# Two transformer blocks on one core: who subtracts, who reads a head, and where block 1's first gelus stand

## The chip, the cores and the metric

The kernel runs on one core of one Trainium2 chip. The metric is the device time of one execution in microseconds. Three runs of the kernel before took 2537.11, 2530.70 and 2521.50 us, a median of 2530.7. The engines are named in the profile as PE (TensorE, with PEld for its weight loads), DVE (VectorE), ACT (ScalarE), POOL (GpSimd) and SP (SyncE, which issues transfers).

## The reference, cut to what matters

Eight sequences of 512 rows by 512 columns go through two blocks. Block 0 quantizes activations and weights; block 1 works on them in full precision.

```python
# block 0, 16 heads of 32 columns
xn = adaln(x, c, g1, w_ada1, b_ada1)
q, k, v = split_heads(bitlinear(xn, w_qkv, b_qkv))
attn = softmax(einsum('bhqd,bhkd->bhqk', q, k) * hd ** -0.5)
o = einsum('bhqk,bhkd->bhqd', attn, v)
x = x + bitlinear(o, w_proj, b_proj)      # bitlinear: act_quant(o) needs each row's absolute maximum
h = gelu(bitlinear(adaln(x, c, ...), w_fc1, b_fc1))
x = x + bitlinear(h, w_fc2, b_fc2)
# block 1, one head of 512 columns
h = film(rmsnorm(x), cond);  x = x + softmax(Q(h) K(h)^T / sqrt(512)) V(h) @ proj
h = film(rmsnorm(x), cond);  x = x + gelu(h @ mlp_w1 + b1) @ mlp_w2 + b2
```

## The kernel before, in words

Every engine has a program of its own, and semaphores tie them together. Each program calls `both(i, j)`: block 0 of sequence i and block 1 of sequence j = i - 1 side by side. It is called nine times: once with block 0 alone, seven times in full, and once with block 1 alone. Nothing is planned at run time: the order on every engine is written out by hand.

Block 0's attention is cut into 64 tiles, four chunks c of four heads, each head with four tiles of 128 keys by 512 queries. The order is a list of 88 slots (c, n): chunk 0 has 24 slots, in which only scores by query run (for the maxima), and chunks 1 to 4 have 16 slots each. In slot (c, n) of the latter, the scores by key of tile e = 16(c - 1) + n are made (`scores_by_key`, line 1035), ScalarE takes their exponential in fp32 (`exponential`, line 1042), and the upper halves of these fp32 words are used as the bf16 high part. The rest, exponential minus high part, is rounded to bf16 by `prob_low` (line 1046) on GpSimd or on VectorE, as the lists `LOW_POOL` and `LOW_DVE` say. Before, VectorE has one of four tiles in the first three chunks and three of four in the last, 24 in all; GpSimd has 40. Scores by query (line 991) and their maxima (`maxima`, VectorE, line 997) run 24 tiles ahead, up to slot (3, 7). Exponentials lie in a ring of eight tiles; every fourth of them waits until the product of the head that used these places is done.

When a head's four tiles are ready, TensorE multiplies them with the head's values (`weigh_values`, line 1061, 32 matmuls of 66 columns), at the slot that `VALUES_AT` gives: `VALUE_LAG` slots after the head's first tile. The two parts of the result and the sum of the exponentials lie in bank 4. VectorE reads them one slot later (`read_head`, lines 1069, 1076 and 1078): reciprocal of the sum, both parts times it, and one part plus the other into y. After the last head it takes absolute maxima of y (`amax0`, line 829) and their scales; ScalarE rounds (`round0`, line 847), VectorE subtracts the constant (line 855), TensorE transposes (line 863), ScalarE copies (line 869) and TensorE projects (`proj0`, line 1087). Then come the norm, whose gain operations are line 814 on VectorE, and block 0's dense layers.

Block 1 uses banks 6 and 7 alone, in turn. Pieces of it are placed between slots: its last scores and projections at chunk 0 and the start of chunk 1, its second norm (`SQUARE_AT`, `NORM_AT`), the turning of the normed rows (`TURN_AT`, lines 1262, 1281, 1291, 1287) and, by `M_AT`, the first six jobs of the list M. M is 16 products of its first dense layer ("fc1") and 16 of its second ("fc2"); each is 12 matmuls of 512 columns (lines 1213 to 1215). A first-layer product is followed by a gelu on ScalarE (line 1430), a bf16 copy on VectorE (line 1436) and its rest on GpSimd (line 1441). There are two buffers for gelus, and a gelu waits for the rest of the one before the last. Exponential and gelu need different tables in ScalarE, so a table load stands before each change. The jobs of M behind the first `M_IN` stand after the attention, mixed with block 0's work. GpSimd also adds block 1's second bias (line 1255) beside four of them.

Of the kernel before, what the change touches and what calls it, by code (L numbers as in the profile page):

```python
# [6 lines left out]
ALU = mybir.AluOpType  # L7
ACT = mybir.ActivationFunctionType
# [5 lines left out]
P = 128  # L14
# [13 lines left out]
MEMORY = 53120  # L28
# [45 lines left out]
LATE_HIGH = {(0, 5): ("q", 2), (0, 9): ("k", 2), (1, 4): ("q", 3), (1, 8): ("k", 3)}  # L74
LATE_LOW = {(0, 7): ("q", 2), (0, 11): ("k", 2), (1, 5): ("q", 3), (1, 9): ("k", 3)}

VALUE_LAG, READ_LAG = ((8, 6, 6, 7), 1)
# [29 lines left out]
LOW_DVE = [e for e in range(KC * HEADS) if (e % 4 == 3 if e < 3 * HEADS else e % 4 != 0)]  # L107
# [68 lines left out]
def two_blocks(nc, a, out):  # L176
# [6 lines left out]
    with ExitStack() as ctx:  # L183
# [73 lines left out]
        o_parts = qk_f[:, 0, 0:TT * 2 * HD].rearrange("p (t s d) -> p t s d", t=TT, s=2)  # L257
# [10 lines left out]
        sum_inv = fp32(2, TT)  # L268
# [56 lines left out]
        o_ok = signal("o_ok", H)  # L325
# [497 lines left out]
        def amax0(dve, i, c, tiles=range(TT)):  # L823
            for t in tiles:
                if c == 1:
                    dve.wait_ge(o_ok.sem, o_ok(i, H))
                else:
                    dve.wait_ge(y_full.sem, y_full(i, c // 2 * TT + t + 1))
# [236 lines left out]

        def read_head(dve, i, h):
            b = ready(dve, plan0, ("o", h), i)
            o = banks[:, b, 0:TT * 2 * LOW].rearrange("p (t s n) -> p t s n", t=TT, s=2)
            dve.reciprocal(sum_inv[:, h % 2], o[:, :, 0, HD]).then_inc(o_small.sem, 1)
            if h > 0:  # L1070
                dve.wait_ge(o_ok.sem, o_ok(i, h))
            else:
                dve.wait_ge(lo_ok.sem, lo_ok(i, 2 * KC - 1))
            dve.wait_ge(o_small.sem, o_small(i, h + 1))
            r = sum_inv[:, h % 2].unsqueeze(2).unsqueeze(3).to_broadcast([P, TT, 2, HD])
            dve.tensor_tensor(o_parts, o[:, :, :, 0:HD], r, ALU.mult).then_inc(free[b].sem, 1)
            done(dve, plan0, ("o", h), i)
# [987 lines left out]
```

## Time and profile before

| | |
|---|---|
| median of three runs | 2530.7 us |
| profiled execution | 2516.55 us |
| its span, first to last instruction | 2514.7 us |
| mean granted TensorE clock | 0.923 |
| PE busy | 2120.9 us, 84% |
| DVE busy | 1683.9 us, 67% |
| ACT busy | 1225.0 us, 49% |
| POOL busy | 768.5 us, 31% |

Busy time is a share of the whole span. The seven full passes of the loop are alike; one of them, whose first exponential starts at 1314.80 us and whose next pass starts its scores at 1563.9 us, is looked at closely below. A granted clock of 1.00 is TensorE's 2.4 GHz, 0.50 is 1.2 GHz, and a number between them is a mean over a stretch.

### The profile page before, as it was taken

To read this page: it belongs to the slowest core of one execution; us is meant where nothing else is said; L and a number is where in the kernel's file an instruction comes from. 1 tells how busy PE (TensorE), PEld (TensorE's weight loads), DVE (VectorE), ACT (ScalarE), POOL (GpSimd) and SP (SyncE) were. 2 spreads that over 40 slices of the span, in tenths; PEclk is the share of its full clock that TensorE was granted. 3 is DMA by queue.
4 is the path that set the end of the run, shared out by engine and by line. 5 is a ranking of instruction groups with operands and counts; after the bars stand their busy time and mean duration, and the time that the engine had idled before them with its cause. 6 is when DMAs were issued, how large, how long until landed. Compare 5 with 4: busy or idle time off the path is not lost.

```text
span 2514.7 us, 40181 instructions
## 1 busy us (share of the span) xinstructions
PE 2120.9 (84%) x13525; PEld 1069.9 (43%) x13525; DVE 1683.9 (67%) x2870; ACT 1225.0 (49%) x2032; POOL 768.5 (31%) x684
## 2 busy tenths in 40 slices
PE   4667688878997799779997899789988898789989
PEld 3424344444444444344444444344444344444434
DVE  4578645877578666877578756967587757866422
ACT  6535334474436554464446544564447444574330
POOL 0135101353125422353125412343136312452112
PEclk8777888989999899989999899989999899999989
DMA  7554111302230122202230213102231213101202
GB/s 276 192 181 164 59 51 34 94 18 76 78 113 22 52 75 96 83 18 76 85 105 22 76 51 121 58 29 82 85 97 31 71 60 124 34 35 51 101 23 95
DMA packets 85507, 200.82 MB, mean 80 GB/s; under 512 B 7604, under 2 KB 48856, under 8 KB 73120
## 3 DMA queue, kind: packets, MB, share of 16 engines
q1 hardware_dynamic: 77512, 174.91, 20.6%
q10 hardware_dynamic: 7776, 23.07, 2.6%
q8 instruction: 127, 2.08, 0.3%
q14 instruction: 92, 0.75, 0.1%
HBM read 161.97 MB, written 35.72 MB: 79 GB/s over the span
## 4 chain that ended last, share of the span: by engine, by line
PE 55%; DVE 17%; issue 13%; ACT 10%; POOL 2%; DMA 2%; ACTq 1%; DVEq 0%; SPq 0%; POOLq 0%
PE banks L1213 10%; PE banks L1214 10%; PE banks L1215 10%; PE banks L1170 5%; PE banks L1105 5%; DVE memory L997 4%; PE banks L1061 4%; DVE memory L1046 2%; ACT memory L1042 2%; DVE memory L814 2%; PE banks L991 2%; PE banks L900 1%; ACT L1042 1%; ACT memory L847 1%; PE banks L1035 1%
## 5 line engine op out<-in xcount | busy, mean ns | idle before, releaser
L1213 PE MATMUL banks<-memory 128*128 128x512 bf16 x1536 | 599.8, 390 | 46.9 <-DVE memory L1463 26.6
L1214 PE MATMUL banks<-memory 128*128 128x512 bf16 x1536 | 597.3, 389 | 0.0
L1215 PE MATMUL banks<-memory 128*128 128x512 bf16 x1536 | 595.3, 388 | 0.0
L1046 POOL TENSOR_TENSOR memory<-memory 128x512 bf16<-128x512 f32 x320 | 356.3, 1125 | 499.2 <-ACT memory L1042 497.4
L1042 ACT ACTIVATE memory<-banks 128x512 f32<-128x512 f32 x512 | 283.9, 597 | 216.7 <-PE banks L1035 179.8
L997 DVE TENSOR_REDUCE memory<-banks 128x1 f32<-128x512 f32 x512 | 330.2, 679 | 52.0 <-PE banks L991 51.0
L1441 POOL TENSOR_TENSOR memory<-memory 128x512 bf16<-128x512 f32 x128 | 163.2, 1275 | 512.5 <-DVE memory L1436 512.5
L991 PE MATMUL banks<-memory 96*128 96x512 bf16 x512 | 197.2, 415 | 103.8 <-DVE memory L997 94.4
L1213 PEld LDWEIGHTS banks<-memory 128*128 128x128 bf16 x1536 | 153.6, 100 | 242.0 <-DVE memory L1463 35.0
L1061 PE MATMUL banks<-memory 128*128 128x66 bf16 x4096 | 177.7, 209 | 76.6 <-DVE memory L1046 67.0
L1215 PEld LDWEIGHTS banks<-memory 128*128 128x128 bf16 x1536 | 153.6, 100 | 192.3 <-issue 19.2
L1035 PE MATMUL banks<-memory 98*128 98x512 bf16 x512 | 202.9, 425 | 30.3 <-ACT memory L1042 23.3
L1214 PEld LDWEIGHTS banks<-memory 128*128 128x128 bf16 x1536 | 153.7, 100 | 174.4 <-issue 16.0
L1061 PEld LDWEIGHTS banks<-memory 128*128 128x128 bf16 x4096 | 165.5, 108 | 120.5 <-issue 109.1
L1046 DVE TENSOR_TENSOR memory<-memory 128x512 bf16<-128x512 f32 x192 | 172.0, 916 | 18.9 <-ACT memory L1042 18.7
L1463 DVE TENSOR_TENSOR memory<-banks,memory 128x512 f32<-128x512 f32 x128 | 88.2, 689 | 141.6 <-PE banks L1215 140.7
L1436 DVE CAST memory<-memory 128x512 bf16<-128x512 f32 x128 | 73.0, 571 | 156.8 <-ACT memory L1430 155.4
L847 ACT ACTIVATE memory<-memory 128x512 f32<-128x512 f32 x96 | 61.3, 710 | 183.4 <-DVE memory L840 177.2
L1162 ACT ACTIVATE memory<-banks 128x512 bf16<-128x512 bf16 x128 | 69.4, 596 | 152.1 <-PE banks L1156 152.1
L1430 ACT ACTIVATE memory<-banks,memory 128x512 f32<-128x512 f32 x128 | 86.9, 684 | 113.2 <-PE banks L1215 112.7
L991 PEld LDWEIGHTS banks<-memory 96*128 96x128 bf16 x512 | 52.2, 102 | 192.1 <-DVE memory L997 152.4
L1170 PE MATMUL banks<-memory 128*128 128x512 fp8e4 x512 | 120.8, 391 | 9.1 <-ACT memory L1162 9.1
(169 smaller groups left out, 3115.9 us busy)
## 6 DMA issues: line engine op xcount, KB each, us to landing
memory<-weight_parts SPq DMA_DIRECT2D x80, 1024.0 KB, 4.9
memory<-head_parts SPq DMA_DIRECT2D x192, 128.0 KB, 2.7
head_parts<-memory SPq DMA_DIRECT2D x64, 256.0 KB, 2.2
weight_parts<-memory ACTq DMA_DIRECT2D x10, 1024.0 KB, 5.0
memory<-in_L_cond_w_fc SPq DMA_DIRECT2D x2, 4096.0 KB, 14.3
memory<-in_x SPq DMA_DIRECT2D x32, 256.0 KB, 3.2
memory<-ada_rows SPq DMA_DIRECT2D x16, 512.0 KB, 4.6
memory<-in_L_cond_mlp_w ACTq DMA_DIRECT2D x8, 1024.0 KB, 8.8
```

The lines of the kernel that those rows point to most:

```text
L991: pe.matmul(banks[:, b], q_stack[0:STACK, c % STACKS, j, t * P:(t + 1) * P], k_stack[0:STACK, c % STACKS, j], start=True, stop=True).then_ ...
L997: dve.tensor_reduce(neg_max[:, c % 2, t, j:j + 1], banks[:, b], AX.X, ALU.max, negate=True).then_inc(free[b].sem, 1)
L1035: pe.matmul(banks[:, b], k_stack[0:rows, c % STACKS, j, kt * P:(kt + 1) * P], q_stack[0:rows, c % STACKS, j], start=True, stop=True).then_ ...
L1042: act.activation(expo[:, e % RING], banks[:, b], ACT.Exp, scale=HEAD_SCALE).then_inc(free[b].sem, 1)
L1046: eng.tensor_tensor(prob_lo[:, e % RING], expo[:, e % RING], prob_hi[:, e % RING], ALU.subtract).then_inc(ok.sem, 1)
L1061: mm = pe.matmul(banks[:, b, at:at + VALUE], part[:, (h * TT + kt) % RING, t * P:(t + 1) * P], values[:, kt, h], start=(kt == 0 and part i ...
L1105: mm = pe.matmul(banks[:, b], xq[:, k, t * P:(t + 1) * P], w0_fc1[:, k, n * D:(n + 1) * D], start=(k == 0), stop=(k == KC - 1))
L1170: mm = pe.matmul(banks[:, b], hid_q[:, f], w0_fc2[:, f], start=(f == 0), stop=(f == FC - 1))
L1213: pe.matmul(bank, lh, rh, start=(k == 0), stop=False)
L1214: pe.matmul(bank, lh, rl, start=False, stop=False)
L1215: mm = pe.matmul(bank, ll, rh, start=False, stop=(k == KC - 1))
L1441: pool.tensor_tensor(hidden_half(g)[:, 1, m], wide[:, f % 2], hidden_half(g)[:, 0, m], ALU.subtract).then_inc(g1_lo.sem, 1)
```

## The change

The lists of rests become contiguous: GpSimd has tiles 0 to 40, VectorE tiles 41 to 63. When a head's product is done, ScalarE copies its high part into y (`copy_head`), one slot after the product; VectorE keeps the reciprocal of the sums in a column for each head and adds the low part out of the bank. After the last head four operations multiply y by the reciprocals of all heads (`divide0`), and the absolute maxima wait for each. Of block 1's list M, two products stand in the attention instead of six, at (4, 5) and (4, 11), and no gelu, bf16 copy or rest of them: these come after the attention on their engines. GpSimd's four additions of block 1's bias stand beside jobs 0 to 3 of M instead of jobs 6 to 9. Some places in the tables shift by one to three slots.

```diff
-LATE_HIGH = {(0, 5): ("q", 2), (0, 9): ("k", 2), (1, 4): ("q", 3), (1, 8): ("k", 3)}
-LATE_LOW = {(0, 7): ("q", 2), (0, 11): ("k", 2), (1, 5): ("q", 3), (1, 9): ("k", 3)}
-VALUE_LAG, READ_LAG = ((8, 6, 6, 7), 1)
+LATE_HIGH = {(0, 5): ('q', 2), (0, 9): ('k', 2), (1, 4): ('q', 3), (1, 9): ('k', 3)}
+LATE_LOW = {(0, 6): ('q', 2), (0, 12): ('k', 2), (1, 5): ('q', 3), (1, 9): ('k', 3)}
+VALUE_LAG, COPY_LAG, READ_LAG = ((6, 7, 7, 7), 1, 1)
+FIRST_DVE = 41
+COPY_AT = {later(at, COPY_LAG): h for at, h in VALUES_AT.items()}
-M_AT = ((3, 0), (3, 4), (3, 8), (3, 12), (4, 0), (4, 6))
+M_AT = ((4, 5), (4, 11))
-TURN_AT = ((2, 4), (2, 6), (2, 8), (2, 10))
+TURN_AT = ((2, 7), (2, 9), (2, 11), (2, 13))
-MAX_AT = {(0, 19): 0, **{(c, 10): c for c in range(1, KC)}}
-HIGH_AT = {(0, 17): 0, **{(c, 9): c for c in range(1, KC)}}
-LOW_AT = {(0, 17): 0, **{(c, 11): c for c in range(1, KC)}}
-LOW_DVE = [e for e in range(KC * HEADS) if (e % 4 == 3 if e < 3 * HEADS else e % 4 != 0)]
+MAX_AT = {(0, 19): 0, (1, 8): 1, (2, 10): 2, (3, 10): 3}
+HIGH_AT = {(0, 17): 0, (1, 9): 1, (2, 10): 2, (3, 9): 3}
+LOW_AT = {(0, 17): 0, (1, 11): 1, (2, 11): 2, (3, 13): 3}
+LOW_DVE = [e for e in range(KC * HEADS) if e >= FIRST_DVE]
...
+        def head_parts(h):
+            o = banks[:, 4, 0:TT * 2 * LOW].rearrange("p (t s n) -> p t s n", t=TT, s=2)
+            return o[:, :, 0, 0:HD], o[:, :, 1, 0:HD], o[:, :, 0, HD], y[:, :, h * HD:(h + 1) * HD]
+
+        def copy_head(act, i, h):
+            ready(act, plan0, ("o", h), i)
+            high, _, _, out = head_parts(h)
+            act.activation(out, high, ACT.Copy).then_inc(o_copied.sem, 1)
+
         def read_head(dve, i, h):
             b = ready(dve, plan0, ("o", h), i)
-            o = banks[:, b, 0:TT * 2 * LOW].rearrange("p (t s n) -> p t s n", t=TT, s=2)
-            dve.reciprocal(sum_inv[:, h % 2], o[:, :, 0, HD]).then_inc(o_small.sem, 1)
...
-            dve.tensor_tensor(o_parts, o[:, :, :, 0:HD], r, ALU.mult).then_inc(free[b].sem, 1)
-            done(dve, plan0, ("o", h), i)
-            dve.tensor_tensor(y[:, :, h * HD:(h + 1) * HD], o_parts[:, :, 0], o_parts[:, :, 1], ALU.add
-                              ).then_inc(o_ok.sem, 1)
+            _, low, total, out = head_parts(h)
+            dve.wait_ge(o_copied.sem, o_copied(i, h + 1))
+            dve.reciprocal(sum_inv[:, :, h], total).then_inc(o_small.sem, 1)
+            dve.tensor_tensor(out, low, out, ALU.add).then_inc(free[b].sem, 1)
+
+        def divide0(dve, i):
+            done(dve, plan0, ("o", H - 1), i)
+            dve.wait_ge(o_small.sem, o_small(i, H))
+            for t in range(TT):
+                r = sum_inv[:, t].unsqueeze(2).to_broadcast([P, H, HD])
+                dve.tensor_tensor(by_head(y[:, t]), by_head(y[:, t]), r, ALU.mult).then_inc(o_ok.sem, 1)
...
                 for n, job in enumerate(M):
-                    if n >= M_IN:
-                        lows1(j, [job])
-                    if j is not None and M_IN <= n < M_IN + TT:
-                        residual_bias1(pool, j, 1, n - M_IN)
+                    lows1(j, [job])
+                    if j is not None and n < TT:
+                        residual_bias1(pool, j, 1, n)
...
+                if i is not None:
+                    for (c, _), h in COPY_AT.items():
+                        if c > KC:
+                            copy_head(act, i, h)
                 join(j, "turn q")
                 join(j, "turn k")
-                highs1(j, M[M_IN:6])
+                highs1(j, M[0:6])
...
                             read_head(dve, i, h)
-                lows1(j, M[M_IN:2])
+                    divide0(dve, i)
+                lows1(j, M[0:2])
```

The tables by which ScalarE, VectorE and GpSimd took block 1's jobs inside the slots lose their entries of M; TensorE's keeps them.

## Rows read from the trace of the kernel before

**Rows 1.** The page: the chain of work that ended last, shares by engine.
```profile
PE 55%; DVE 17%; issue 13%; ACT 10%; POOL 2%; DMA 2%; ACTq 1%; DVEq 0%; SPq 0%; POOLq 0%
```

**Rows 2.** Stretches, one pass: length, PE, PEld, DVE, ACT, POOL busy (count), clock, DMA.
```profile
1314.80:1336.37 21.57, 16.05 (x154) 7.98 (x153) 19.55 (x35) 14.04 (x30) 13.84 (x14) 1.00 0.10 33
1336.37:1347.26 10.89, 8.78 (x92) 5.88 (x90) 9.02 (x15) 7.66 (x15) 6.47 (x7) 0.84 0.23 60
1347.26:1365.59 18.33, 12.98 (x102) 7.03 (x102) 13.86 (x26) 7.28 (x14) 6.63 (x6) 0.81 0.00 1
1365.59:1378.00 12.41, 11.09 (x104) 5.48 (x102) 10.82 (x19) 10.85 (x14) 8.30 (x8) 1.00 0.00 1
1378.00:1389.86 11.86, 10.43 (x102) 5.31 (x101) 5.48 (x12) 11.32 (x16) 8.47 (x8) 1.00 0.28 90
1389.86:1400.61 10.75, 7.34 (x91) 3.95 (x90) 8.10 (x15) 10.63 (x15) 5.80 (x5) 1.00 0.01 2
1400.61:1410.43 9.82, 6.44 (x101) 4.80 (x100) 6.90 (x12) 4.13 (x8) 4.04 (x3) 0.68 0.01 2
1410.43:1420.36 9.93, 8.09 (x41) 3.65 (x40) 6.66 (x17) 5.74 (x9) 0.68 (x1) 0.80 0.15 49
1423.97:1443.90 19.93, 17.44 (x76) 7.44 (x75) 17.08 (x26) 4.54 (x9) 7.38 (x7) 0.91 0.39 132
1443.90:1563.90 120.00, 117.37 (x653) 57.46 (x651) 74.40 (x126) 58.35 (x99) 28.74 (x27) 1.00 0.22 78
```

**Rows 3.** Groups by line in 1314.80 to 1410.43: count, busy us, mean ns, idle before.
```profile
L1046 POOL TENSOR_TENSOR memory<-memory 128x512 bf16<-128x512 f32 x40 | 43.6, 1101 | 61.7 <-ACT memory L1042 61.4
L1042 ACT ACTIVATE memory<-banks 128x512 f32<-128x512 f32 x64 | 35.5, 596 | 25.3 <-PE banks L1035 20.4 <-PE banks L1061 4.6
L997 DVE TENSOR_REDUCE memory<-banks 128x1 f32<-128x512 f32 x40 | 26.1, 679 | 5.9 <-PE banks L991 5.9
L1046 DVE TENSOR_TENSOR memory<-memory 128x512 bf16<-128x512 f32 x24 | 21.9, 931 | 2.6 <-ACT memory L1042 2.6
...
L1430 ACT ACT_TABLE_LOAD x6 | 7.7, 1283 | 0.1
L1042 ACT ACT_TABLE_LOAD x6 | 7.7, 1283 | 0.1
L1078 DVE TENSOR_TENSOR memory<-memory 128x128 f32<-128x128 f32 x15 | 7.2, 479 | 0.5
...
L1430 ACT ACTIVATE memory<-banks,memory 128x512 f32<-128x512 f32 x6 | 4.1, 687 | 0.1
...
L1227 ACT ACTIVATION_READ_ACCUMULATOR memory<-memory 128x1 f32 x4 | 0.8, 190 | 0.0
```

**Rows 4.** Single lines over the whole span: duration ns min/median/max, first and last start.
```profile
L1046 POOL TENSOR_TENSOR memory<-memory x320: 1028/1039/2930, 168.0 to 2236.6; 128x512 bf16<-128x512 f32 x160
L1046 DVE TENSOR_TENSOR memory<-memory x192: 669/681/1640, 172.9 to 2240.0; 128x512 bf16<-128x512 f32 x192
...
L1069 DVE RECIPROCAL memory<-banks x128: 164/173/184, 180.4 to 2243.2; 128x4 f32<-128x4 f32 x128
...
L1076 DVE TENSOR_TENSOR memory<-banks,memory x128: 423/424/426, 180.7 to 2243.4; 128x256 f32<-128x256 f32 x128
...
L1078 DVE TENSOR_TENSOR memory<-memory x128: 291/292/1190, 181.2 to 2243.9; 128x128 f32<-128x128 f32 x128
...
L814 DVE SCALAR_TENSOR_TENSOR memory<-memory x64: 743/752/1755, 107.0 to 2264.6; 128x512 f32<-128x512 f32 x64
```

**Rows 5.** Timeline behind the attention of that pass: start us, us, engine, line, operation [idle before].
```profile
1406.21 1.13 PE L1061 MATMUL banks<-memory 128*128 128x66 bf16 x32 [2.23 <-DVE memory L1046]
1408.49 1.94 PE L1061 MATMUL banks<-memory 128*128 128x66 bf16 x32 [1.15 <-DVE memory L1076]
...
1420.36 3.61 PE L1087 MATMUL banks<-memory 128*128 128x512 fp8e4 x16 [1.84 <-ACT memory L869]
...
1427.20 6.37 DVE L814 SCALAR_TENSOR_TENSOR memory<-memory 128x512 f32<-128x512 f32 x4
```

More of the change, by code:

```diff
@@ L27 @@
 STACK = 3 * HD
-MEMORY = 53120
+MEMORY = 53184
 N_BIAS = 36
@@ L256, in two_blocks @@
         prob_lo = x0.rearrange("p t d -> p (t d)").bitcast(BF16).rearrange("p (r n) -> p r n", r=RING)
-        o_parts = qk_f[:, 0, 0:TT * 2 * HD].rearrange("p (t s d) -> p t s d", t=TT, s=2)
         ada = fp32(2, D)
@@ L267, in two_blocks @@
         neg_max = fp32(2, TT, G)
-        sum_inv = fp32(2, TT)
+        sum_inv = fp32(TT, H)
         nmax1, nb1, sum1, suminv1 = fp32(TT), fp32(TT), fp32(TT), fp32(TT)
@@ L324, in two_blocks @@
         o_small = signal("o_small", H)
-        o_ok = signal("o_ok", H)
+        o_copied = signal("o_copied", H)
+        o_ok = signal("o_ok", TT)
         h_act = signal("h_act", 16)
@@ L825, in amax0 @@
                 if c == 1:
-                    dve.wait_ge(o_ok.sem, o_ok(i, H))
+                    dve.wait_ge(o_ok.sem, o_ok(i, t + 1))
                 else:
@@ L1486, in two_blocks @@
         DVE_AT = place(*s_p(S_AT, PT_READ), *((at, ("proj", t)) for t, at in enumerate(PROJ_READ)),
-                       *((later(at, 2), ("low", k)) for k, at in enumerate(TURN_AT)),
-                       *((later(at, 2), job) for at, job in zip(M_AT, M)))
+                       *((later(at, 2), ("low", k)) for k, at in enumerate(TURN_AT)))
         ACT_AT = place(*s_p(S_AT, PT_READ), *((at, ("square", t)) for t, at in enumerate(SQUARE_AT)),
@@ L1491, in two_blocks @@
                        *((at, ("full", k)) for k, at in enumerate(TURN_AT)),
-                       *((later(at, 1), ("film", k)) for k, at in enumerate(TURN_AT)),
-                       *((later(at, 1), job) for at, job in zip(M_AT, M)))
-        POOL_AT = place(*((later(at, 2), job) for at, job in zip(M_AT, M)))
+                       *((later(at, 1), ("film", k)) for k, at in enumerate(TURN_AT)))
         CUTS = [(14, 14, 15, 16), (16, 17, 18, 19), (19, 20, 21, 22), (22, 23, 24, 25), (25, 26, 27, 27)]
@@ L1598, in both @@
                             rstd_of1(pool, j, 1)
-                        lows1(j, POOL_AT.get((c + 1, n), []))
                 for n, job in enumerate(M):
-                    if n >= M_IN:
-                        lows1(j, [job])
-                    if j is not None and M_IN <= n < M_IN + TT:
-                        residual_bias1(pool, j, 1, n - M_IN)
+                    lows1(j, [job])
+                    if j is not None and n < TT:
+                        residual_bias1(pool, j, 1, n)
                     if i is not None and n == 6:
@@ L1699, in both @@
                         qk_high(act, i, late, part)
+                    if i is not None and (c, n) in COPY_AT:
+                        copy_head(act, i, COPY_AT[c, n])
                     if i is not None and c > 0:
@@ L1859, in both @@
                             read_head(dve, i, h)
-                lows1(j, M[M_IN:2])
+                    divide0(dve, i)
+                lows1(j, M[0:2])
                 join(j, "turn q")
-                lows1(j, M[max(M_IN, 2):3])
+                lows1(j, M[2:3])
                 if i is not None:
@@ L1865, in both @@
                 join(j, "turn k")
-                lows1(j, M[max(M_IN, 3):4])
+                lows1(j, M[3:4])
                 if i is not None:
@@ L1869, in both @@
                     scales0(dve, i, 1, 1)
-                lows1(j, M[max(M_IN, 4):6])
+                lows1(j, M[4:6])
                 if i is not None:
                     whole0(dve, i, 1)
-                lows1(j, M[max(M_IN, 6):8])
+                lows1(j, M[6:8])
                 if i is not None:
```

6 lines of the change are left out of this document (removed).

## The prediction

> **What bounds the kernel now.** I began with the chain of work that ended last [rows 1]: TensorE carries over half of it, VectorE and ScalarE take turns in the rest, so no single engine is the answer and the stages must be read apart. Each of the seven full passes of the loop has three stages: an opening in which block 1's queries and values and the first scores run, the attention of block 0, and a long stretch of dense products. The table by stretches [rows 2] shows one pass. The reader should compare each stretch's length with its busiest engine. In the last stretch (120.0 us) TensorE is busy for 117.4: any product that lands there costs its full time. In the attention, 95.6 us in seven rows (21.57 + 10.89 + 18.33 + 12.41 + 11.86 + 10.75 + 9.82), nobody is full throughout: VectorE leads in the first three rows (19.6 of 21.6, 9.0 of 10.9, 13.9 of 18.3), and ScalarE in the three that hold gelus (10.9 of 12.4 though TensorE has 11.1, 11.3 of 11.9, 10.6 of 10.8).
>
> The groups of that window [rows 3] say what fills them. VectorE does 40 maxima at 0.68 us and 24 rests at 0.93 us on average; a rest takes 0.67 at least and 1.64 at most [rows 4]. ScalarE spends 12 x 1.283 = 15.4 us on table loads for six gelus of 0.69 us. GpSimd does 40 rests in 43.6 us and sleeps for 61.7.
>
> **The rests.** GpSimd keeps 41 rests instead of 40, VectorE 23 instead of 24, so the totals are unchanged; the order is not. In key chunks 0 and 1 (rows one to three of the stages) VectorE loses its eight rests, 8 x 0.93 = 7.4 us, while it still has 32 maxima. GpSimd then takes one tile per slot: 41 x 1.04 [rows 4] = 42.6 us, 45.1 at the mean of 1.10, plus 1.3 for small operations of the norm (the first row's 13.84 of 14 instructions, less 12 rests [rows 2]). That is its floor up to the 41st exponential, which starts 63.2 us behind the first today (the first four rows). From the 42nd VectorE has no maxima left, and 23 x 0.67 = 15.4 us of rests.
>
> **The reading of a head.** Today a head costs VectorE a reciprocal of 0.17, a product of both parts of 0.42 [rows 4] and an addition of 0.48 on average [rows 3]. The addition has two operands in SBUF and runs from 0.29 to 1.19; the product, with one operand in PSUM, stays within 0.423 and 0.426 in 128 cases beside the same GpSimd work [rows 4]. The new addition, 128x128 with one operand in PSUM, is between 0.29 and 0.42; I take 0.29, the row with its number of elements. A head falls from 1.07 to 0.46: 0.61 x 16 = 9.8 us less VectorE. ScalarE gains a 128x128 copy out of PSUM per head: between a read of one element, 0.19 [rows 3], and an exponential of 512 columns, 0.60; a quarter of the way gives 0.29, so 4.7 us per pass. ScalarE has room only because the loads go. The copy stands in front of the next exponential and waits for the head's product to end (1.13 us at the full clock [rows 5]); behind it are the exponentials, then TensorE, which has two banks for scores. I charge nothing for that alone where an exponential already fills half of the wait, and keep it as a rival.
>
> **The division.** Four operations of 128x512 after the last head; the nearest row is a rest, as wide and with two operands in SBUF, 0.67 to 1.64 [rows 4], and near 0.67 as GpSimd has nothing to do then: 2.7 us before the absolute maxima, but by then TensorE has six products to cover it (below), so it costs nothing; without that cover it would be 2.7 per pass.
>
> **The gelus and products of block 1.** Twelve loads leave the attention, 15.4 us of ScalarE, and one is needed behind it. On ScalarE's loads a rule bears: the table-load row is 1.28 long, and the next operation starts right behind it, so twelve cost 15.4. The Trainium skill (ScalarE: Activation LUTs, "What ACT_TABLE_LOAD costs") adds a drain of about 1.38 us to each switch, 2.66 in all; by it twelve would be 31.9 and the pass could shed up to 16.5 more. The trace disagrees: the row of 10.75 us with 10.63 busy [rows 2] has no room for drains.
>
> Of six products four leave the attention. One product is 12 matmuls. Sixteen of the same width take 3.61 at the full clock [rows 5], 0.215 from one to the next: 2.6 us a product, 10.3 for four. Two remain, (4,5) and (4,11), and occupy both banks of block 1 until ScalarE's gelus, which now stand behind all exponentials and the last copy. So TensorE can't begin the third product until: copy 0.3, load 1.28, gelu 0.69, and 0.3 that I add for the hand-overs, together 2.6 us idle. The chain behind it is in VectorE's queue: reads, division (end at +3.7 after the last product of values), then the rounding-down copies of the first three gelus, two absolute maxima, a fourth copy, two more maxima, the small operations, +11. ScalarE's rounding waits for its six gelus, whose last needs the sixth product: 2.6 + 4 x 2.6 + 0.7 = +13.7. Rounded rows reach TensorE from +14.9 to +17, and its own six products end at +18.2. They cover each other. Block 0's projection starts about +20, where it starts now at +9.93. The load that stood in front of it (the 1.84 us wait [rows 5]) is gone, worth 1.5. By this count it comes 10 later; I take 11.4 = 10.3 + 2.6 - 1.5, as the first product may run at half clock, as today.
>
> GpSimd's four additions of block 1's bias move from beside VectorE's gain operations to before them. Today these take 6.37 us for four [rows 5], where 0.75 each [rows 4] makes 3.0; TensorE waits behind and the clock falls (0.91 in 1423.97 to 1443.90 [rows 2]). Six products of 2.6 are 15.5 of that stretch's 19.93; I take 3.9 back, since both the wait and its slow clock go. SyncE's weight loads wait for the products that moved; each has over 8 us until it is needed, and its queue waits for nothing earlier than today.
>
> **The sum of one pass, row by row [rows 2].** 21.57 becomes 21.2: VectorE falls to about 15, but TensorE takes one more head into it and GpSimd needs 17.9. 10.89 becomes 9.3 (GpSimd 8.3 plus a start). 18.33 becomes 13.5: the product of about 3.5 us in front of its last score goes, VectorE sheds two rests and shrinks its heads, but all four turns of the norm are now in it, which gives ScalarE about 11 us and VectorE as much with contention. 12.41 becomes 9.3, GpSimd at 8.3. 11.86 becomes 8.0: VectorE eight operations of 0.67 and two heads, 6.3, and a chain through three engines. 10.75 becomes 8.5 and 9.82 becomes 9.5, each with a product and the rests on VectorE alone. Sum 79.3: 16.3 less. Behind it +11.4 - 3.9 = +7.5. Net -8.8 a pass, -62 in seven. The first pass has no block 1 in it: its attention sheds contention and gains the division, I take -4 (between +3 and -10). The closing pass has no attention; 0. **Total -66.** The profiled execution took 2516.6 us, so 2451 by its own measure; it is 14 us under the median of 2530.7, to which I apply the same difference: 2465.
>
> **Rivals.**
> *The slots flow freely.* If the first 41 exponentials come near GpSimd's floor (52 us to there) and VectorE's 23 rests run unbroken, the attention ends at about 75.5, 20 less, and the stage behind costs only 5.5 more. Then (-20 + 5.5) x 7 - 6 = -107: 2424. For it: VectorE's lead in the first rows is removed. Against: no stretch of today runs at its busiest engine where three alternate (13.9 of 18.3). The lowest bound, all floors at once (44 + 21 us), would be some -180.
>
> *Copies hold the exponentials.* If each of 13 copies inside the slots keeps ScalarE for 1.13 less half an exponential, plus 0.29, it is 0.9 each, 11.6 per pass, and only 4.7 of the 16.3 remain: (-4.7 + 7.5) x 7 - 4 = +16, or 2547, within 1% of now. For it: ScalarE already waited for head products in this window, 4.6 us [rows 3]. Against: these waits were for the ring's old head, and TensorE is two scores ahead.
>
> *Slower: TensorE's clock.* Place: slots (2,8) to the end. Today the clock there is at its full 2.4 GHz while block 1's products stand between the scores (1.00 in three rows) and falls to a granted 0.68 once they are gone [rows 2]. Half clock makes a matmul step 0.43 instead of 0.215 and a head's product 1.94 instead of 1.13 [rows 5]. Slots of chunk 2 then need 16 x 0.43 + 3.9 = 10.8 for 9.3 assumed, chunk 3 with its product 12.4 for 8.5, the end 13 for 9.5; with 2 more in the third row, 0.4 in the fifth and 2.5 in the first product behind, 14 a pass. Then (-8.8 + 14) x 7 - 4 = +32: 2563. It decides from about two thirds of these losses on, a mean granted clock near 0.65 from (2,8). Against: at half clock TensorE is busy nearly all the time, and behind the attention the mean of 0.80 over 9.93 us [rows 2] leaves at most 4.0 us at half clock before dense products have it full again.
> The Trainium skill (TensorE: Matmul & The Clock Gate, "What's actually happening") says that throttled is the default and activity releases it; by it thinning the attention speaks for this rival, and the 0.68 row agrees.
>
> *It changes nothing.* Were the loads caused by copies and not by gelus they would stay; but gelu and exponential rows have six loads each for six gelus [rows 3]. Time as now.
>
> **Chances.** Forecast 0.60, free flow 0.13, copies 0.15, clock 0.09, nothing 0.03. A difference of 1% is about what a measurement can tell. Faster by over 1%: 0.71 (nearly all of the first two); within: 0.18; slower: 0.11, the clock and the far end of the copies. The range goes from below free flow, 2410, to 2540, which leaves out the clock and about half of the copies.
>
> **What would show it.** Table loads fall from twelve to none between the first and last exponential of a pass; VectorE's additions with a PSUM operand stay at 0.3; GpSimd is over nine tenths busy to the 41st exponential; a wait of about 2.6 us on a gelu stands behind the last head; the gain operations take 3 us for four; the granted clock stays over 0.8 in chunk 2. I am wrong if the 41st exponential comes later than 58 us after the first, if the stage behind the attention grows by over 11 us, or if ScalarE's waits for head products exceed 8 us a pass.

## The result, and the profile after

The changed kernel takes 2401.5 us (median, 2398.9 to 2408.9), the kernel before 2533.9 on the same chip: a ratio of 0.949, interval 0.944 to 0.953. The profiled execution took 2402.7 us where that of before took 2516.6: 114 us less, against the 66 I forecast. The time lies 8 us under my range.

First the chain of work that ended last, to hold against [rows 1]:

```profile
PE 63%; DVE 12%; POOL 8%; issue 7%; ACT 6%; DMA 2%; ACTq 1%; SPq 0%; DVEq 0%; POOLq 0%
```

ScalarE and VectorE lost ground in it, and GpSimd rose from 2% to 8%. The same pass by stretches (columns as in [rows 2]), first exponential to last product of values in eight lines; the first two of them answer to the first of before:

```profile
1261.30:1271.35 10.05, 9.09 (x68) 4.25 (x66) 7.75 (x15) 6.05 (x13) 7.51 (x8) 1.00 0.00 0
1271.35:1281.44 10.09, 6.52 (x84) 3.63 (x84) 7.62 (x17) 8.77 (x21) 9.30 (x10) 1.00 0.20 66
1281.44:1289.04 7.60, 6.72 (x86) 4.03 (x87) 5.23 (x10) 6.53 (x15) 7.60 (x9) 1.00 0.37 91
1289.04:1299.99 10.95, 8.99 (x97) 5.90 (x96) 10.83 (x20) 9.04 (x20) 10.95 (x10) 0.86 0.01 2
1299.99:1306.89 6.90, 6.37 (x80) 3.12 (x78) 5.18 (x12) 5.12 (x11) 6.76 (x8) 0.97 0.00 0
1306.89:1314.63 7.74, 5.10 (x76) 3.11 (x77) 6.61 (x14) 5.29 (x12) 3.24 (x3) 0.96 0.02 4
1314.63:1322.32 7.69, 7.69 (x86) 4.84 (x84) 4.65 (x10) 4.50 (x11) 0.00 (x0) 0.81 0.01 2
1322.32:1331.66 9.34, 7.28 (x115) 4.64 (x113) 6.59 (x16) 4.74 (x11) 0.00 (x0) 1.00 0.01 3
...
1331.66:1352.87 21.21, 18.31 (x89) 8.36 (x90) 14.05 (x26) 9.94 (x16) 13.17 (x11) 0.92 0.17 53
...
1356.30:1374.60 18.30, 16.84 (x90) 7.81 (x89) 14.76 (x28) 5.91 (x12) 3.59 (x5) 1.00 0.43 143
```

The attention takes 70.4 us where it took 95.6. Up to the 41st exponential (five lines) GpSimd is busy for 42.1 of 45.6 us, and fully in two lines, the third and the fourth, in the fourth together with VectorE (10.8 of 10.95). The groups of that window, for [rows 3], with the count in front of the bar and busy us, mean ns and idle time behind it:

```profile
L1048 POOL TENSOR_TENSOR memory<-memory 128x512 bf16<-128x512 f32 x41 | 44.2, 1112 | 30.7 <-ACT memory L1044 30.6
L1044 ACT ACTIVATE memory<-banks 128x512 f32<-128x512 f32 x64 | 36.0, 595 | 18.8 <-PE banks L1037 18.5
L999 DVE TENSOR_REDUCE memory<-banks 128x1 f32<-128x512 f32 x40 | 25.6, 679 | 2.6 <-PE banks L993 2.6
...
L1048 DVE TENSOR_TENSOR memory<-memory 128x512 bf16<-128x512 f32 x23 | 15.7, 727 | 3.4 <-ACT memory L1044 3.4
...
L1076 ACT ACTIVATE memory<-banks 128x128 f32<-128x128 f32 x15 | 4.1, 275 | 3.9 <-PE banks L1063 3.8
L1083 DVE TENSOR_TENSOR memory<-banks,memory 128x128 f32<-128x128 f32 x15 | 3.8, 257 | 0.0
```

No table load is left among them. VectorE's rests fell from 931 to 727 ns, since GpSimd sleeps beside most of them: before, 13 of a pass's 24 overlap with an instruction on GpSimd and take 1140 ns in the mean, the others 678; after, two of 23 overlap. Behind the attention the timeline shows the forecast gap, a table load in front of the first gelu and TensorE waiting for it:

```profile
1330.51 1.14 PE L1063 MATMUL banks<-memory 128*128 128x66 bf16 x32 [1.47 <-DVE memory L1083]
1331.68 0.28 ACT L1076 ACTIVATE memory<-banks 128x128 f32<-128x128 f32 x1 [2.33 <-PE banks L1063]
1331.98 1.28 ACT L1441 ACT_TABLE_LOAD   x1
...
1332.38 2.49 DVE L1090 TENSOR_TENSOR memory<-memory 128x512 f32<-128x512 f32 x4
1333.27 1.27 ACT L1441 ACTIVATE memory<-banks,memory 128x512 f32<-128x512 f32 x2
1334.02 0.39 PE L1224 MATMUL banks<-memory 128*128 128x512 bf16 x1 [2.37 <-ACT memory L1441]
```

Over the seven full passes the two traces divide as follows (means, worked out from the starts of the first instruction of each stage):

| us a pass | before | after | measured | forecast |
|---|---|---|---|---|
| pass start to first exponential | 28.50 | 29.57 | +1.1 | 0 |
| attention | 96.33 | 69.48 | **-26.9** | -16.3 |
| to block 0's projection | 9.93 | 21.46 | +11.5 | +11.4 |
| projection to first dense product | 25.59 | 21.74 | -3.9 | -3.9 |
| dense products to next pass | 135.58 | 137.77 | +2.2 | 0 |

That is -15.9 a pass, -111.4 in seven; -4.4 in the first pass (forecast -4), and 1.9 more ahead of it: -114. (The last row's mean holds the closing pass, itself 0.3 longer.)

### The profile page after: what moved, and what is told of

Its sections match the earlier page's. It is cut to its first block, busy times and chain, and to the rows that moved or that the text cites. A ratio compares the mean times of both kernels' runs of the same rounds, so it can differ in the third digit from the quotient of the medians.

```text
span 2400.9 us, 40046 instructions
## 1 busy us (share of the span) xinstructions
PE 2065.7 (86%) x13525; PEld 1045.8 (44%) x13525; DVE 1560.9 (65%) x2766; ACT 1146.5 (48%) x2076; POOL 749.3 (31%) x692
## 4 chain that ended last, share of the span: by engine, by line
PE 63%; DVE 12%; POOL 8%; issue 7%; ACT 6%; DMA 2%; ACTq 1%; SPq 0%; DVEq 0%; POOLq 0%
PE banks L1224 13%; PE banks L1225 12%; PE banks L1226 12%; POOL memory L1048 7%; PE banks L1181 5%; PE banks L1116 5%; PE banks L1063 2%; DVE memory L999 2%; PE banks L902 2%; PE banks L1037 2%; PE banks L761 1%; PE banks L1098 1%; PE banks L993 1%; DVE memory L816 1%; PE banks L1167 1%
## 5 line engine op out<-in xcount | busy, mean ns | idle before, releaser
L1048 POOL TENSOR_TENSOR memory<-memory 128x512 bf16<-128x512 f32 x328 | 358.8, 1126 | 250.3 <-ACT memory L1044 249.8
L1452 POOL TENSOR_TENSOR memory<-memory 128x512 bf16<-128x512 f32 x128 | 149.6, 1168 | 611.6 <-DVE memory L1447 611.6
L1224 PEld LDWEIGHTS banks<-memory 128*128 128x128 bf16 x1536 | 153.0, 100 | 248.8 <-issue 21.6
L1226 PEld LDWEIGHTS banks<-memory 128*128 128x128 bf16 x1536 | 153.3, 100 | 190.7 <-issue 16.5
L1225 PEld LDWEIGHTS banks<-memory 128*128 128x128 bf16 x1536 | 153.2, 100 | 174.0 <-issue 14.9
L1037 PE MATMUL banks<-memory 98*128 98x512 bf16 x512 | 190.6, 403 | 27.4 <-DMA memory<-memory 14.2
L1063 PE MATMUL banks<-memory 128*128 128x66 bf16 x4096 | 158.4, 200 | 22.7 <-DVE memory L1083 11.2
L1063 PEld LDWEIGHTS banks<-memory 128*128 128x128 bf16 x4096 | 150.5, 102 | 59.4 <-issue 26.1
L1447 DVE CAST memory<-memory 128x512 bf16<-128x512 f32 x128 | 64.2, 506 | 136.3 <-ACT memory L1441 135.1
L1048 DVE TENSOR_TENSOR memory<-memory 128x512 bf16<-128x512 f32 x184 | 125.5, 728 | 20.6 <-ACT memory L1044 20.6
L1266 POOL TENSOR_TENSOR memory<-memory 128x512 f32<-128x512 f32 x64 | 80.8, 1278 | 133.7 <-DVE memory L878 126.4
```

Source lines behind the costliest of these rows:

```text
L1037: pe.matmul(banks[:, b], k_stack[0:rows, c % STACKS, j, kt * P:(kt + 1) * P], q_stack[0:rows, c % STACKS, j], start=True, stop=True).then_ ...
L1048: eng.tensor_tensor(prob_lo[:, e % RING], expo[:, e % RING], prob_hi[:, e % RING], ALU.subtract).then_inc(ok.sem, 1)
L1063: mm = pe.matmul(banks[:, b, at:at + VALUE], part[:, (h * TT + kt) % RING, t * P:(t + 1) * P], values[:, kt, h], start=(kt == 0 and part i ...
L1224: pe.matmul(bank, lh, rh, start=(k == 0), stop=False)
L1225: pe.matmul(bank, lh, rl, start=False, stop=False)
L1226: mm = pe.matmul(bank, ll, rh, start=False, stop=(k == KC - 1))
```

## The experiments

Each of the four parts was done alone, three of them were undone alone (the shifted slots were not), and then the sizes that were in dispute were moved. "Attention" is the mean of the seven passes, to be held against 96.3 before and 69.5 after. The changed kernel run again (e16, at the end) has 70.2, so differences under 1 us there mean little.

**One part alone, on the kernel before.** Only the two lists of rests (e1):

```diff
-LOW_DVE = [e for e in range(KC * HEADS) if (e % 4 == 3 if e < 3 * HEADS else e % 4 != 0)]
+LOW_DVE = [e for e in range(KC * HEADS) if e >= 41]
```

> The kernel before with one edit: GpSimd has rests 0 to 40, VectorE 41 to 63. Theory (the parts need each other: GpSimd's chain becomes the floor only once VectorE and ScalarE are both relieved): the first two chunks shrink by about 5 us a pass, the last two stay with ScalarE's table loads, so 30 to 50 us off 2534. Rival (each part is worth its own share, they add): some 45 us, a third of 132. Rival (the order of the rests is the whole change): 100 us or more.

Measured 2466.6 us, ratio 0.974; attention 88.5. That is some 68 us, more than the theory and the sharing rival gave it; the 41st exponential comes 6.7 us a pass earlier, and the rows with gelus get no shorter, as the theory said.

Only the reading of a head (e2: `copy_head`, the new `read_head`, `divide0`), copies one slot after the products:

```diff
+COPY_AT = {later(at, 1): h for at, h in VALUES_AT.items()}
```

> The kernel before with one edit: ScalarE copies a head's high part one slot after its product, VectorE adds the low part, one division at the end. Theory (parts need each other): VectorE is relieved by 0.6 us a head, but the division stands in front of the absolute maxima with no cover, 2 to 3 us a pass; 5 to 25 us off 2534. Rival (shares add): 45 us. Rival (copies hold the exponentials): 10 us or more slower.

Measured 2542.7 us, ratio 1.005 (1.002 to 1.009): slightly slower, which none of the three had. Attention 94.1, but 2.1 more to the projection (the division, here with no products to cover it), 1.5 more behind it, and 2.0 and 1.0 more in the dense stage and the opening. VectorE has 9.6 us a pass less work in the attention, but it waits there for ScalarE's copies, in front of the reciprocals:

```profile
L1082 DVE RECIPROCAL memory<-banks x128: 163/185/186, 179.6 to 2269.6; 128x4 f32<-128x4 f32 x128
its engine sat idle before it (us, times) until:
  ACT memory L1076: 147.9, 113
```

In the attention that is 16.3 us a pass, where VectorE sat idle for 1.8 us in front of its reciprocals before and for 8.1 after.

Only block 1's products and gelus (e3):

```diff
-M_AT = ((3, 0), (3, 4), (3, 8), (3, 12), (4, 0), (4, 6))
+M_AT = ((4, 5), (4, 11))
```

> The kernel before with one edit: two products of block 1 in the attention instead of six, no gelu in it, and GpSimd's bias additions beside the first jobs. Theory (parts need each other): the attention loses some 12 us a pass and the stage behind it gains 7.5, so 20 to 45 us off 2534, with VectorE as the next limit. Rival (shares add): 45 us. Rival (the table loads are the whole change): 100 us or more.

Measured 2465.5 us, ratio 0.973; attention 85.7, to the projection 18.3. The two stages moved about as the theory said (-10.7 for -12, +8.3 for +7.5), but it left out the 3.9 us of the gain operations, which come with this part; the total, 70 us, is above the theory's and the sharing rival's.

The shifted slots alone (e15: `LATE_HIGH`, `LATE_LOW`, `VALUE_LAG`, `TURN_AT`, `MAX_AT`, `HIGH_AT`, `LOW_AT` as in the diff):

> The kernel before with the shifted slots alone (the tables of late parts, turns, maxima and the lags of the value products as in after); rests, heads, division and gelu as before. Theory (the slots only fit the other three parts, which alone sum to 130 of the 132 us): 2518 to 2542 us, attention 94 to 97 us a pass, stage to the projection 9.9 us. Rival (the slots themselves keep scores from waiting, and each of the three parts alone was measured with the help of them or lacks them): attention 88 to 92 us, 2480 to 2505 us. Third way (earlier values of the first heads make the second row's heads wait): 2545 to 2570 us.

Measured 2501.1 us, ratio 0.991 (0.987 to 0.995); attention 92.9. The theory falls: the slots are worth 3.5 us a pass by themselves. The time is the rival's, the attention a little above what it said. The row with the turns went from 18.33 to 15.56.

The four parts alone give -2.6, +0.5, -2.7 and -0.9%, together -5.7 against -5.1 for the whole change; in the attention -7.9, -2.2, -10.7 and -3.5, together -24.2 of -26.9. They add up to about the whole. Undone (next), three of them are worth 4.8, 9.4 and 17.0 us in the attention, not 7.9, 2.2 and 10.7: they do interact, in both directions, and the good sum hides it.

**One part undone, in the changed kernel.** The old lists of rests (e4):

```diff
-LOW_DVE = [e for e in range(KC * HEADS) if e >= FIRST_DVE]
+LOW_DVE = [e for e in range(KC * HEADS) if (e % 4 == 3 if e < 3 * HEADS else e % 4 != 0)]
```

> The changed kernel with one edit undone: the lists of rests as before (VectorE one of four, then three of four). Theory (parts need each other): more is lost than this part brings alone, 60 to 90 us over 2402. Rival (shares add): as much as it brings alone. Rival (order of the rests is nothing): within 10 us of 2402.

Measured 2440.8 us, ratio 0.964; attention 74.3: the rests, added last, bring 4.8, and some 39 us in all. That is less than alone (68), so neither the theory (60 to 90) nor the rivals had it.

The old reading of a head (e5: no copy on ScalarE, no division at the end):

```diff
-            dve.tensor_tensor(out, low, out, ALU.add).then_inc(free[b].sem, 1)
...
+            dve.tensor_tensor(o_parts, o[:, :, :, 0:HD], r, ALU.mult).then_inc(free[b].sem, 1)
```

> The changed kernel with one edit undone: VectorE reads both parts of each head and scales them, no copy on ScalarE, no division at the end. Theory A (once GpSimd carries all early rests, a head's addition with two operands in SBUF waits for GpSimd, so the new reading pays only there): the first 41 exponentials take 4 us a pass longer, the stage behind the attention 2 us less, in sum 0 to 25 us over 2402. Theory B (the new reading is a loss everywhere, as alone): 8 to 25 us under 2402. Either way the opening and the dense stage, which are 3 us a pass longer in both kernels that read heads the new way, tell whether the new reading causes that.

Measured 2415.9 us, ratio 0.959; attention 78.9. What is worth 2.2 us in the attention alone is worth 9.4 with the others in place: theory A, with larger sizes (the 41st exponential comes 6.8 us later). But the stage to the projection is 17.1 us here and 21.5 in the changed kernel. Without the last head's copy, ScalarE does its table load and the first gelus beside the last head's product, and TensorE has no gap. So the new reading gives 9.4 us a pass in the attention and takes 4.4 behind it; another 2.0 come back in the opening and the dense stage.

The gelus and the four products back in the attention (e6):

```diff
-M_AT = ((4, 5), (4, 11))
+M_AT = ((3, 0), (3, 4), (3, 8), (3, 12), (4, 0), (4, 6))
```

> The changed kernel with one edit undone: six products of block 1 with their gelus, bf16 copies and rests inside the attention, at (3,0), (3,4), (3,8), (3,12), (4,0), (4,6), and GpSimd's bias additions at the seventh to tenth job. Theory (shares add): 60 to 75 us over 2402, with 12 table loads back, the last three rows of the attention at 12 us again and the stage behind it 11 us shorter. Rival (GpSimd is now the bound and the loads would hide behind it): less than 30 us over.

Measured 2492.0 us, ratio 0.990; attention 86.4. The stretches of its rows with gelus:

```profile
1338.92:1351.26 12.34, 11.23 (x104) 5.40 (x102) 6.41 (x14) 11.19 (x16) 8.87 (x9) 1.00 0.01 2
1351.26:1362.80 11.54, 10.42 (x100) 5.08 (x99) 5.36 (x11) 11.42 (x18) 5.71 (x5) 1.00 0.17 50
1362.80:1373.92 11.12, 7.53 (x87) 4.00 (x87) 7.45 (x18) 11.00 (x18) 2.05 (x2) 1.00 0.11 44
```

ScalarE is busy for 91, 99 and 99% of them, 5.1 us of it four table loads in each; VectorE for 52, 46 and 67%. In the last two ScalarE is the bound; in the first TensorE, with two products in it, is as busy (11.2). The same rows take 11.86 and 10.75 us before and 11.86 and 10.76 in e1, where VectorE is busy for 5.5 and 8.1, and for 7.2 and 8.3 us: its work didn't set their length. The loads and the products left these rows together; no run parts them. The theory had the direction and the row lengths, but the 90 us over the changed kernel are more than its 60 to 75.

**Who sets the pace up to the 41st exponential?** Three rests of the first rows given to VectorE (e7):

```diff
-LOW_DVE = [e for e in range(KC * HEADS) if e >= FIRST_DVE]
+LOW_DVE = [e for e in range(KC * HEADS) if e >= FIRST_DVE or e in (5, 13, 21)]
```

> The changed kernel with one edit: rests 5, 13 and 21 go from GpSimd to VectorE, 38 and 26. Theory (GpSimd's chain of 41 rests, 1.1 us each, is what now sets the end of the first 41 exponentials, and VectorE has 4.8 us of slack in the first row): 3 us a pass earlier, 15 to 25 us under 2402. Rival (GpSimd is busy but follows; VectorE's maxima or TensorE set the pace): no difference or a few us slower, since VectorE works more beside its maxima.

Measured 2416.6 us, ratio 0.960: the theory falls. The attention is 70.3 and the 41st exponential comes 1.3 us later, not 3 earlier; the other loss is in the dense stage, 1.4 longer, for a reason that lies in the number or place of VectorE's instructions (last section). The line in which VectorE has one such rest and GpSimd one less is longer than the 10.09 us of after, with VectorE busy for 9.1 us instead of 7.6 and the clock at 0.86:

```profile
1276.79:1288.89 12.10, 7.99 (x84) 4.45 (x84) 9.07 (x21) 9.02 (x20) 8.86 (x10) 0.86 0.18 58
```

The border between the two lists at 33 and at 49 instead of 41 (`FIRST_DVE`; e8 and e9):

> The changed kernel with one edit: VectorE takes over the rests at tile 33 instead of 41, while eight of its maxima are still to come. Theory (VectorE in its order, not GpSimd's work alone, sets the pace wherever maxima and rests meet): the row from slot (3,0) grows from 7 to about 10 us, 10 to 30 us over 2402. Rival (GpSimd's 41 rests are the floor): eight rests less there save 2 us a pass or more, 10 to 20 us under 2402.

> The changed kernel with one edit: VectorE takes over the rests at tile 49 instead of 41, behind its last maximum by two heads. Theory (the end of the first 41 is GpSimd's, at 1.1 us a tile, and behind it TensorE and VectorE pace at 0.95 a tile): about 1.5 us a pass more, 5 to 20 us over 2402. Rival (it makes no difference who has tiles 41 to 48): within 4 us.

Measured 2393.2 and 2395.3 us (0.947, 0.948); attention 70.9 and 72.5, where the changed kernel has 69.5 and, run again, 70.2: 41 is better than 49 there, and not clearly better than 33. With 33 the row from slot (3,0) does grow, from 7.3 to 9.2 us, as the theory said, but rows around it shrink. Both totals contradict their theories, and neither rival's range holds them. That both kernels are not slower than the changed one comes from outside the attention (last section).

Rests left out altogether, on the improved version below (e13):

```diff
-LOW_POOL = [e for e in range(KC * HEADS) if e not in LOW_DVE]
+LOW_POOL = [e for e in range(KC * HEADS) if e not in LOW_DVE and e not in (13, 21, 29)]
```

> e11_more_waits with the rests of the exponentials 13, 21 and 29 not computed in any pass (the products of values with them take an older rest), one out of the second, third and fourth row each; all else as in e11_more_waits, which took 2370.7 us. In the trace of after a rest on GpSimd takes 1.04 us when undisturbed. Theory (GpSimd's own work is what the rows wait for up to the 41st exponential): the 41st exponential comes 2.5 to 3.5 us earlier than the 48.5 us of e11_more_waits, the attention takes 68 to 69 us instead of 71.2, and the kernel 2346 to 2353 us. Rival (GpSimd is full because the others keep step with it, the bound is TensorE's scores and VectorE's in-order list): the 41st exponential moves by under 1 us, the attention by under 1 us, the kernel takes 2364 to 2377 us.

Measured 2367.9 us, against 2370.6 of the same kernel with them, as the rival had it. 3.1 us less work for GpSimd moved the mean start of the 41st exponential from 47.9 to 47.2 us behind the first and the attention from 71.1 to 70.8. (In the pass shown it came 1.8 us earlier, the largest of the seven differences, though this row is not shorter.) One row of each kernel, the one with the turns, without the three rests and then with them:

```profile
1270.63:1280.65 10.02, 7.68 (x97) 4.91 (x96) 9.77 (x17) 8.99 (x20) 7.42 (x8) 1.00 0.01 2
```

```profile
1272.67:1282.05 9.38, 7.67 (x97) 4.90 (x96) 9.13 (x17) 8.99 (x19) 9.38 (x9) 1.00 0.01 3
```

GpSimd is full in the second and has 2.6 us to spare in the first, which is no shorter, since VectorE is full in both. So GpSimd, though it has the largest total up to the 41st exponential, does not alone hold the others.

**What is given back outside the attention.** Two gelus of block 1 ahead of the last head's copy, so that TensorE gets a bank sooner (e10):

```diff
+                highs1(j, M[0:2])
+                if i is not None:
+                    copy_head(act, i, H - 1)
...
-                highs1(j, M[0:6])
+                highs1(j, M[2:6])
```

> The changed kernel with one edit: on ScalarE the first two gelus of block 1 stand before the copy of the last head, not behind it. Theory (TensorE's 2.4 us of idle time behind the attention is the table load and the gelu that free a bank, and its half clock afterwards, 1.5 us, comes from that gap): the gap closes, 2.4 to 4 us a pass, 15 to 27 us under 2402. Rival (the gap only moves: the last head's copy, and with it the division and the absolute maxima, comes later and the projection of block 0 waits for the rounding): within 5 us of 2402.

Measured 2374.7 us, ratio 0.943 (0.936 to 0.950). To the projection 17.9 us instead of 21.5, and all else as in the changed kernel: the 2.4 us gap and more is recovered, as the theory said.

The same with three repeated waits, already fulfilled, in VectorE's list at each head (e11):

```diff
             dve.wait_ge(o_copied.sem, o_copied(i, h + 1))
+            dve.wait_ge(o_copied.sem, o_copied(i, h + 1))
+            dve.wait_ge(o_copied.sem, o_copied(i, h + 1))
+            dve.wait_ge(o_copied.sem, o_copied(i, h + 1))
```

> The kernel with the first two gelus ahead of the last copy (2375), and VectorE's wait for the copy of a head written four times instead of once, the three others met at once. VectorE then has about as many instructions in its program as with the old reading of heads. Theory (the idle 1 to 2 us of VectorE at the start of a pass, which only the kernels with the new reading show, comes from fetching its program, and depends on its length and position): the idle time goes or moves, up to 2 us a pass either way. Rival (it comes from a semaphore or from where the tiles lie in memory): it stays as it is.

Measured 2370.7 us, ratio 0.938. The two stages outside (dense and opening) fall from 167.6 to 164.9 us a pass, so the idle time went, as the theory said; the attention grows by 1.3. Only where `sum_inv` lies in memory, moved behind the other small tiles, the waits not added (e12):

> The kernel with the first two gelus ahead of the last copy (2375), and the tile with the reciprocals of the sums laid behind all others in memory, so that every other tile lies where it lay in the kernel before. Theory (the idle time at the start of a pass comes from the place of the small tiles): it goes, 2 us a pass, 2361. Rival (program fetch): it stays, within 4 us of 2375.

Measured 2373.1 us, ratio 0.939, and the two stages stay at 166.3: the place of that tile is not the cause.

Last, the improved version (the kernel with both edits) and the changed kernel on one chip (e14, e16):

> The version of e11_more_waits again, in five rounds: after with two parts of the gelu ahead of the last head's copy and three waits added to VectorE's list. It took 2370.7 us in one round, against 2401.5 of after. Theory (both gains are real and add: 3.9 us a pass of stage, 2 of idle time of VectorE, less 1.5 that the attention is longer): 2366 to 2376 us, ratio to before 0.934 to 0.942, and 1.2 to 1.4% under after. Rival (one of them is the chip's own scatter): 2380 to 2395 us.

> The changed kernel unaltered, beside e14_best on the same chip: 2397 to 2408 us, ratio to before 0.946 to 0.951. If it lands under 2385 us, the gain of e14_best over it is scatter between chips.

Measured 2370.6 (0.939, 0.936 to 0.943) and 2400.8 us (0.951, 0.947 to 0.955): 1.3% between them, as expected. The improved version beats both kernels.

## Why the prediction was wrong

The direction stood, and so did the prices of the single operations; the sum for the attention did not, a part was priced at nothing, and a loss was not foreseen. Step by step:

- **Table loads, gelus: right.** None is left between the exponentials, and e6 shows ScalarE as the bound of two of the three rows that held them.
- **The stage behind the attention: right**, +11.5 for +11.4, with a gap of 2.37 us for my 2.6, and four divisions of 2.49 us in all, covered by TensorE's products. Their price without cover, 2.1 a pass in e2, was put at 2.7. That the sum fits to 0.1 is in part luck: at a mean clock of 0.92 over 21.2 us, half clock cost about 1.7 us (an estimate from these two numbers), which I had named but not counted. My own sign of being wrong, a growth of over 11 us here, came true; set below my forecast of 11.4, it could tell nothing.
- **The gain operations: right**, -3.9; four take 3.35 us instead of 6.37, and the stretch now runs at a full clock, where [rows 2] has 0.91.
- **The new reading: right in its prices**, 0.257 us for the addition and 0.275 for the copy, where I took 0.29 twice.
- **The failed step is the sum of one pass, row by row:** 79.3 us where 69.5 came. In the profiled pass, rows one to four took 20.1, 7.6, 11.0 and 6.9 us where I had 21.2, 9.3, 13.5 and 9.3: 45.6 for 53.3. I gave each row its fullest engine "plus a start" and added these up. No such start was paid. Rows two and four are even shorter than the 8.3 us that I gave GpSimd for their eight rests, and row three is as long as its fullest engines are busy (10.95). GpSimd's list isn't cut at the rows: a rest is wanted only three to seven slots after its tile, so GpSimd can fall behind in one row (in this pass it starts a rest up to 1.6 us after its exponential's end) and catch up in a row where another engine leads. The text had 42.6 plus 1.3 = 43.9 as the floor; the 41st exponential came at 45.7 in the mean, and the 9 us that I laid on top were mostly not paid. The floor was itself not strict, since GpSimd had done 38 of the 41 rests by then, and e13 shows that GpSimd alone doesn't set this time. For the free flow I even named 52, above that floor by 8, for no reason that a row gave. The last three rows were 1.2 us shorter than forecast in this pass, and 2.5 where the seventh line takes 6.37 us, as in five passes.
- **A part priced at nothing:** the shifted slots. I counted the turns' move as a load on the third row and the rest as free; e15 has them at -3.5 a pass when done alone, a third of what is missing between my -16.3 and the -26.9.
- **A loss that I didn't see:** 3.3 us a pass in the dense stage and the opening, +23 in all. About 2.7 of it goes with three repeated waits (last section).

Of the rivals, the free flow was the case, and went further than I let it: -26.9 in the attention for -20, but +7.7 net behind it (11.53 less 3.85) for the 5.5 that I gave it there, without reason. The copies don't hold the exponentials: ScalarE waited 3.8 us for head products in the whole window, under the 4.6 of [rows 3]. What they cost stands on VectorE, 8.1 us a pass of waiting for copies, which I hadn't counted. I had also added up that rival wrongly: 1.13 less 0.30 plus 0.29 is 1.12 us a copy, not 0.9, so 14.6 a pass, and 2567 us for it instead of 2547. The clock didn't fall: 0.81 to 1.00 in all rows, 0.95 in the mean over the attention where the rows of [rows 2] give 0.91. What I had missed there is that the attention got denser for TensorE, not thinner: 57.8 us busy in 70.4, 82%, where [rows 2] add up to 73.1 in 95.6, 76%. The Trainium skill (TensorE: Matmul & The Clock Gate, "What's actually happening"), by which activity releases the clock, agrees with that; I had applied it to fewer products and forgotten the shorter time.

Why the head's new reading is worth four times as much once the other parts are in is answered only in part. Alone (e2), its gain on VectorE, 9.6 us of work a pass, goes into waits for the copies, 16.3 us; with the others in place these waits are 8.1. Why the copies come so late in e2 was not taken apart. ScalarE has 15.4 us of table loads there, but VectorE waits in the rows without loads too.

## What to carry to other kernels

Where engines with separate lists take turns as the bound, don't add up the maxima of short rows: work out each engine's total over the stretch within which its work may lag (here all rows up to the 41st tile), take the largest, and add only the waits that the buffers force. Here that gives 42.1 us for 45.6, nearer than the row sum of 53.3. It is a lower estimate and doesn't say who holds whom: with 3.1 us less on the engine with the largest total, 0.7 were gained (e13). A part done alone can hide what it is worth (the head's reading: 2.2 us alone, 9.4 undone), so test from both ends. And look at the stages the change doesn't touch: here they gave back 3.3 of 19.2 us a pass.

## What the runs showed of the hardware that I had not expected

In the dense stage VectorE works out the low part of block 1's queries (bank plus bias, less the high part), and TensorE waits for it. First the changed kernel, then the one with three repeated waits (e11), the same operation in both (duration min/median/max; idle time before it; who waited):

```profile
L1351 DVE SCALAR_TENSOR_TENSOR memory<-banks,memory x32: 739/749/752, 407.8 to 2256.0; 128x512 bf16<-128x512 f32 x32
its engine sat idle before it (us, times) until:
  ACT memory L1342: 17.8, 12
  issue: 3.4, 2
who waited for it (us, times):
  PEld banks L1224: 18.1, 9
  PE banks L1224: 14.6, 6
```

```profile
L1354 DVE SCALAR_TENSOR_TENSOR memory<-banks,memory x32: 737/744/752, 402.3 to 2223.1; 128x512 bf16<-128x512 f32 x32
its engine sat idle before it (us, times) until:
  ACT memory L1345: 9.2, 4
who waited for it (us, times):
  PEld banks L1227: 10.1, 14
  PE banks L1227: 5.2, 6
```

The four times that e11 keeps are in the closing pass and are the same in every kernel. The others begin with one pause in each of the six passes before it: VectorE is idle for 1.2 to 1.9 us in front of the pass's first of these operations and begins it 0.5 to 1.2 us after ScalarE's part, to which the profile puts the wait down, has ended. In e7, whose VectorE has three rests more in its list, the pause stands two operations earlier, between gain operations of which the third waits for nothing ("issue"). First the changed kernel, then e7, one pass each:

```profile
1457.84 2.74 DVE L816 SCALAR_TENSOR_TENSOR memory<-memory 128x512 f32<-128x512 f32 x4 [2.63 <-POOL memory L801]
1461.82 0.75 DVE L1351 SCALAR_TENSOR_TENSOR memory<-banks,memory 128x512 bf16<-128x512 f32 x1 [1.24 <-ACT memory L1342]
```

```profile
1467.60 1.41 DVE L816 SCALAR_TENSOR_TENSOR memory<-memory 128x512 f32<-128x512 f32 x2 [2.91 <-issue]
1468.93 0.74 DVE L1351 SCALAR_TENSOR_TENSOR memory<-banks,memory 128x512 bf16<-128x512 f32 x1
```

In the kernels that have the pause (the changed one, e2, e4, e6, e7, e10, e12) TensorE waits 14.6 to 24.3 us for the query line in all, in the others (the kernel before, e1, e3, e5, e8, e9, e11) 5.1 to 8.2. Between the changed kernel, e8 and e9 nothing differs but which engine has eight of the rests, and between e10 and e11 nothing but 48 waits a pass: so the number or place of VectorE's instructions decides, not their work.

The transfers in the same traces point to what the pause waits for. VectorE's program is a loop over the passes, and its branch comes 80.0 us behind the first dense product of the pass in every run. About 6 us later, 85.5 to 86.6 us behind that product, a packet of 8 KB starts in one of the DMA queues for instructions (q14). In all 48 pauses (six in each of eight profiled runs, the changed kernel counted twice) VectorE goes on 1.73 to 1.87 us after the start of this packet, although the packet itself starts at times that differ by 1.1 us. The packet also comes in the ten runs without a pause. This fits a loop whose next piece of program arrives late, and which notices it only when its instructions reach the end of the piece before. No run moved the packet or the branch by itself, so it is argued from the timing and not proven.

With the pause gone the six dense stages are back at 118.8 us (e11; 118.7 before, 121.2 in the changed kernel). The opening stays 0.8 longer than before, and that I did not place.
